# A decoder layer on one core: one exponential moved up on ScalarE, one wait added on GpSimd, one reduction a step later on VectorE

## The reference

```
x = x + self_attention(layernorm(x))          # three softmaxes a row, averaged
x = x + cross_attention(layernorm(x), ctx)    # 16 heads, mask added to the scores
x = x + ffn(layernorm(x))                     # two layers on values rounded to 127 steps
```

## Time and profile before

| what | value |
|---|---|
| median of 3 runs | 1637.55 us (1637.49 to 1640.61) |
| the profiled execution | 1638.86 us, its span 1637.1 us |
| PE busy | 1522.7 us, 93% |
| DVE busy | 1427.2 us, 87% |
| ACT busy | 1218.9 us, 74% |
| POOL busy | 1067.1 us, 65% |
| DMA, over the span | 46 GB/s |
| ACT exponentials, L1174 and L1176 | 256 each, mean 600 and 610 ns |
| POOL exp_lo, L658 | 256, mean 1185 ns |
| POOL idle before exp_lo, waiting for exponentials | 82.8 us |
| DVE waits for normalised x2 before L1516 | 12.0 us in 32 waits |

### The profile page before, as it was taken

How to read it: one execution, slowest core, us unless ns; L and a number is a source line. 1 busy time by engine, 2 the same in 40 slices (tenths; PEclk the granted TensorE clock), 3 DMA queues, 4 the chain that set the end, 5 groups by cost and what they waited for, 6 DMA issues and landing times.

```text
span 1637.1 us, 52303 instructions
## 1 busy us (share of the span) xinstructions
PE 1522.7 (93%) x15938; PEld 1221.6 (75%) x15946; DVE 1427.2 (87%) x6188; ACT 1218.9 (74%) x2497; POOL 1067.1 (65%) x1168
## 2 busy tenths in 40 slices
PE   6589999999999999999999999999999999779897
PEld 5468888888888888888888888888888887532465
DVE  4779999999999999999999999999999996669786
ACT  4767777777777777777777777777777777469875
POOL 3467777777777777777777777777777777642000
PEclk9889999999999999999999999999999999889999
DMA  6000000000000000000000000000000000245154
GB/s 215 4 15 30 29 29 29 29 24 26 29 29 29 29 29 29 29 29 28 23 28 29 29 24 28 29 29 29 29 29 29 29 22 17 91 119 138 39 180 168
DMA packets 92292, 74.67 MB, mean 46 GB/s; under 512 B 20832, under 2 KB 91744, under 8 KB 92256
## 3 DMA queue, kind: packets, MB, share of 16 engines
q1 hardware_dynamic: 91296, 74.08, 14.7%
q10 hardware_dynamic: 960, 0.13, 0.1%
HBM read 45.36 MB, written 25.17 MB: 43 GB/s over the span
## 4 chain that ended last, share of the span: by engine, by line
PE 59%; DVE 18%; ACT 10%; issue 8%; POOL 3%; ACTq 1%; DVEq 1%; DMA 0%; POOLq 0%; SPq 0%
PE banks L124 16%; PE banks L127 13%; PE banks L128 12%; PE banks L914 5%; DVE tile_max L2126 4%; PE banks L934 3%; DVE xn L1342 2%; ACT kv_copy L1154 2%; PE banks L958 2%; ACT normed L1191 2%; PE banks L2030 2%; PE banks L806 2%; DVE g_t_half L1363 2%; DVE stats L1507 1%; POOL rstd L671 1%
## 5 line engine op out<-in xcount | busy, mean ns | idle before, releaser
L658 POOL TENSOR_TENSOR exp_t<-exp_copy,exp_t 128x512 f16<-128x512 f32 x256 | 303.4, 1185 | 141.9 <-ACT exp_copy L1176 82.8
L652 POOL TENSOR_TENSOR shifted<-scores,score_max 128x512 f32<-128x512 f32 x256 | 266.3, 1046 | 131.9 <-DVE score_max L1387 127.2
L1387 DVE CUSTOM_DVE_ANT_0 scores<-banks,mask 128x128 f32<-128x128 f32 x1024 | 232.7, 286 | 6.2 <-PE banks L914 2.9
L1151 ACT ACTIVATE q_t<-banks 128x512 f16<-128x512 f32 x128 | 77.2, 603 | 131.9 <-PE banks L128 131.7
L644 POOL TENSOR_TENSOR v_nat<-kv_copy,v_nat 128x512 f16<-128x512 f32 x128 | 143.8, 1123 | 46.1 <-ACT kv_copy L1154 46.0
L934 PE MATMUL banks<-ident,shifted 128*128 128x128 f32 x1024 | 153.6, 278 | 19.2 <-ACT exp_copy L1176 17.5
L1174 ACT ACTIVATE exp_t<-banks 128x512 f16<-128x512 f32 x256 | 153.6, 600 | 18.5 <-PE banks L934 15.6
L1176 ACT ACTIVATE exp_copy<-banks 128x512 f32<-128x512 f32 x256 | 156.1, 610 | 0.0
L1154 ACT ACTIVATE kv_copy<-banks 128x512 f32<-128x512 f32 x252 | 150.2, 596 | 0.0
L644 POOL TENSOR_TENSOR k_t<-kv_copy,k_t 128x512 f16<-128x512 f32 x124 | 143.9, 1161 | 0.0
L934 PEld LDWEIGHTS banks<-ident,shifted 128*128 128x128 f32 x1024 | 115.3, 142 | 27.6 <-issue 20.6
(11 more groups left out here) (276 smaller groups left out, 5059.3 us busy)
## 6 DMA issues: line engine op xcount, KB each, us to landing
x_in<-in_x_dram SPq DMA_DIRECT2D x32, 256.0 KB, 2.6
ctx_in<-in_ctx_dram SPq DMA_DIRECT2D x32, 256.0 KB, 2.6
x_residual<-x SPq DMA_DIRECT2D x64, 128.0 KB, 1.7
x_normalised<-normed SPq DMA_DIRECT2D x32, 256.0 KB, 2.1
shared<-x_normalised SPq DMA_DIRECT2D x8, 1024.0 KB, 6.9
shared<-x_residual SPq DMA_DIRECT2D x16, 512.0 KB, 3.7
out_dram<-shared SPq DMA_DIRECT2D x16, 512.0 KB, 2.9
mask<-in_fside_Bx1xSxS_dram SPq DMA_DIRECT2D x64, 64.0 KB, 1.9
```

The source lines that it names most:

```text
L652: pool.tensor_tensor(shifted[:, q % 2], scores[:, q % 2], score_max[:, q % 2, :].unsqueeze(2).to_broadcast([P, QUAD, P]), ALU.subtract).th ...
L658: pool.tensor_tensor(exp_t[:, q % 2, LO], exp_copy[:, q % 2], exp_t[:, q % 2, HI], ALU.subtract).then_inc(exp_split, 1)
L1151: op = act.activation(hilo(dst, *at)[HI], src, ACT.Copy)
L1387: op = dve.tensor_tensor_reduce(scores[:, q % 2, h, :], sc_bank(q)[:, tile(h)], mask[:, b, :], 1.0, NEG, ALU.add, ALU.max, score_max[:, q ...
```

## The change

Three edits, in the lists of three engines:

- ScalarE: exponential(3) of the pair before stands ahead of hi(K2) instead of behind it.
- GpSimd: ahead of exp_lo(5), and so ahead of all that follows, it waits for `xn1_ready` of pair i, which VectorE raises at the end of the second instruction that normalises x1. Only in bodies with a front and a back (1 to 31).
- VectorE: `largest_of_x2` of pair i-1 at the end of body i becomes `largest_of_x2` of pair i-2 behind divide(0) in body i. Body 1 has nothing to reduce and is written out ahead of the loop, which now runs from 2 to 30; body 32 reduces pair 30 there and pair 31 at its end.

```diff
--- before.py
+++ after.py
@@ -696,6 +696,9 @@
             if back:
                 shift(6, i - 1)
+                if front:
+
+                    pool.wait_ge(xn1_ready, i + 1)
                 exp_lo(5, i - 1)
                 shift(7, i - 1)
@@ -1203,10 +1206,11 @@
             if early:
                 weights_of["cross_hi"](act, 8, 12)
+            if back:
+                exponential(3, i - 1)
             if front and not early:
                 hi(J_K2, i)
             if back:
-                exponential(3, i - 1)
                 heads_hi(0, i - 1)
                 exponential(4, i - 1)
@@ -1355,7 +1359,7 @@
-        def body(i, front, back, ahead, early=False):
+        def body(i, front, back, ahead, early=False, far=True):
@@ -1557,6 +1561,9 @@
                     row_sums(0, i - 1)
                     divide(0, i - 1)
+                if back and far:
+
+                    largest_of_x2(i - 2)
                 if back and not front:
                     ffn_of["weight_peak"](dve, 0)
@@ -1686,7 +1693,7 @@
                 if front:
                     add_mask(4, i)
-                if back:
+                if back and not front:
                     largest_of_x2(i - 1)
@@ -1696,7 +1703,8 @@
         body(0, True, False, True, True)
-        with dve.Fori(1, PAIRS - 1) as i:
+        body(1, True, True, True, far=False)
+        with dve.Fori(2, PAIRS - 1) as i:
             body(i, True, True, True)
```

## The result

The changed kernel takes 1687.5 us (median of 6 runs, 1686.04 to 1689.37) against 1638.43 for the kernel before: ratio 1.0297, 95% interval 1.0284 to 1.0311. It is slower, as forecast, but by 49 us where 23 were forecast, and outside the range (1638 to 1684). The profiled execution takes 1686.04 us, its span is 1684.2.

What follows compares the result with a forecast made beforehand. TensorE, busy 1229 of 1262 us in the pair loop, bounds it; +0.85 a pair times 30 gives +25.5, with pair 31 and the last body +23.5 on 1638.86: 1662.4, median 1661 us, range 1638 to 1684.

Steps and rivals of the forecast that it cites:

- Keys(1), -0.36: TensorE before keys(1): VectorE's reduction no longer delays the low part of the first probabilities, so keys(1) starts 0.36 us earlier.
- The transposes of quad 5, -0.80: TensorE before quad 5: earlier exponentials free its bank, so its transposes start at 656.11 instead of 656.91.
- The port takes x's normalisation: GpSimd's low half of quad 3 holds VectorE's normalisation of the next x: +1.44 us; x transposes +1.22.
- x's low half, +0.22: fold_value(1) on TensorE waits for x's low half from VectorE, adding 0.22 us to a pair.
- Quad 4, -0.27: GpSimd's low half of quad 4 moves 0.8 us ahead, so the 0.27 us lost before weigh(4) vanishes.
- weigh(5), +0.15: Quad 5's low half on GpSimd runs later, so TensorE's weigh(5) waits, giving 0.15 us back.
- raw_scores: TensorE before raw_scores: x1's normalisation takes 0.73 instead of 1.83 us, so the 0.42 stall goes.
- The sum without the clock: Terms over one pair: +1.22 + 0.22 - 0.27 - 0.42 + 0.15 = +0.90 us, taken as +0.85.
- if weigh(5) doesn't wait: Variant of the pair's sum in which quad 5's low half does not delay TensorE: 0.75 us.
- The extra unrolled body: The body written out on VectorE's queue: costed at 0, as no compute instruction is added in all.
- The clock: Rival, chance 0.16: TensorE's stall lowers the granted clock, 1.7 us in a fifth to two fifths of pairs, 1671 to 1681.
- -0.42 + 0.15: GpSimd's wait for x1's normalisation: raw_scores' 0.42 us stall removed, 0.15 given back at weigh(5).

Runs made afterwards that it cites:

- edit 1: Only VectorE's move of largest_of_x2 behind quad 0's division, against the kernel before: 1636.61 us, ratio 0.9985.
- the filled stall: The changed kernel, with TensorE doing quad 5's four transposes four times in steady pairs: 1659.12 us, ratio 1.0125 to the kernel before.
- edit 2 alone: Only ScalarE's exponential(3) moved ahead of hi(K2), against the kernel before: 1655.41 us, ratio 1.0102.
- edits 2 and 3: ScalarE's moved exponential(3) and GpSimd's wait for xn1_ready, without VectorE's move, against the kernel before: 1660.32 us, ratio 1.0138.
- Edit 3: Only GpSimd's wait for xn1_ready ahead of exp_lo(5), against the kernel before: 1629.46 us, ratio 0.9941.
- edits 1 and 2: VectorE's moved largest_of_x2 and ScalarE's moved exponential(3), without GpSimd's wait, against the kernel before: 1698.36 us, ratio 1.0362.

## Why the prediction was right in kind and wrong in size

- **Keys(1), -0.36: right in place, too small.** The low part of the probabilities moved up and the gap went. Keys(1) starts at 671.13, 0.03 behind the matmul ahead of it and not 0.11 as forecast; that is 649.71 in the time of before, -0.44, and what follows is 0.47 earlier.
- **The transposes of quad 5, -0.80: too small as well.** They start at 677.33, which is 655.91 in the time of before (656.11 forecast): -1.00. The forecast let them start 0.12 behind weigh(2), and they start 0.03 behind it.
- **The port takes x's normalisation: right.** 2.39 us, done at 679.98, in the time of before 658.56 (forecast 658.55); two instructions held, GpSimd ahead at 677.52. The transposes of x are at 680.12, +1.32 (forecast +1.22). TensorE, early at one end and late at the other, stands for 2.15 us and not 1.89 (656.71 to 658.60 in the forecast).
- **x's low half, +0.22: only 0.06.** fold_value(1) is at +1.38 (forecast +1.44). It follows weigh(3) by 0.36 us in both kernels, so it doesn't wait for the low half; the 0.06 come in at K3's start behind the stall.
- **Quad 4, -0.27: right.** weigh(4) is at +1.11 (+1.17).
- **weigh(5), +0.15: there.** Its first row before is

```profile
664.06 0.20 PE L114 MATMUL banks<-v_nat,exp_t 128*128 128x66 f16 x1
```

After, it starts at 686.72, +1.24, where weigh(4) was at +1.11. GpSimd's low half of quad 5 ended at 686.59, so the delay between the two was 0.13 us and not the 0.22 forecast. raw_scores is at +0.74: it gains 0.50 there where 0.42 was forecast.

- **The sum without the clock: 0.72, forecast 0.85.** 1.32 + 0.06 - 0.27 + 0.13 - 0.50 leaves 0.74 at raw_scores, 0.72 at the end of the pair. That it is near the 0.75 given for "if weigh(5) doesn't wait" is luck: weigh(5) does wait. 29 x 0.72 = 21 us. The extra unrolled body was costed at 0; the first period, which begins in it, is 0.33 us longer than the short ones (43.12), and no kernel without edit 1 shows that.
- **The clock: the step that failed.** The sum left it out; it stood as a rival with a chance of 0.16 and 1.7 us for a fifth to two fifths of the pairs. The price of one was near (44.30 - 42.79 = 1.51). The share was 18 of 29, above the upper end of the rival too, and 18 x 1.51 = 27 us; the filled stall measures 28. The two terms make 48 us, which is what the 29 periods grew by (48.6); the medians differ by 49. I set the chance low with the argument that the stall is single with dense work on both sides; but the evidence that I showed, behind the stalls of pair 31, spoke for the fall. The stall was sized short as well (1.89, measured 2.15), and its size matters: 1.68 us cost no fall with edit 2 alone.
- **What was never weighed: that two gains make one loss.** Edit 1 moves TensorE 0.47 up to a wait whose end it does not move (offset 14.64 with it and 14.62 without). So it saves nothing there and makes the stall 2.15 instead of 1.67. With edits 2 and 3 in, edit 1 costs 1687.5 - 1660.3 = 27 us, and all of it is clock, since the short period is 42.79 with it and without; alone it gains 2.
- **Edit 3** was costed as -0.42 + 0.15 in this kernel. On top of edit 2 it shows +0.09 (42.70 and 42.79; ratios 1.0102 and 1.0138): x1's normalisation is free in any case, since the late exponentials hold GpSimd back, and what is left is its price, weigh(5) at offset 21.23 instead of 21.01. It does help alone (-0.37). In the changed kernel its wait is 86.9 us of GpSimd's idle time, most of which costs nothing.

The Trainium skill (SBUF — State Buffer, "Who interferes with whom") says that tensor_reduce on this chip never contends with GpSimd. The trace agrees: before, the reduction of x2 started at 649.21, inside a shift on GpSimd that ran from 649.05 to 650.09, and took 0.69 us, no longer than the 0.67 in its new place.

## What to carry to other kernels

When a wait is removed, look at what its owner does instead of waiting: the engine that stood still may have left a shared port free for another's short, urgent instruction. Before moving work up, find the instruction that sets the end of the next wait; if the move doesn't touch it, the gain becomes a longer stall, and on TensorE a longer stall may cost the clock too, as here between 1.68 and 2.15 us. Where stalls near those that went before a fall of the clock are forecast in every period, the fall belongs in the sum and not among the rivals.

## What the runs showed of the hardware

- A small difference of one stall decided over the clock here. Stalls of 1.67 and 1.68 us once a pair cost it in none of 29 periods (edits 2 and 3, edit 2); stalls of 2.15 us in 18 (all three) and in 28 (edits 1 and 2), so the length alone doesn't decide; the same wait with 1.95 us of transposes ahead of it instead of 0.64, and so 0.84 us idle, in none (the stall filled). One fall costs 1.5 us of a pair.
- VectorE's two normalising instructions take 0.40 us each when free, and up to 1.25 each when a GpSimd instruction with SBUF operands is under way (1.23 and 1.24 in the changed kernel). In the changed kernel the first starts at 677.59 behind GpSimd's 677.52 and ends at 678.82, when GpSimd's has ended (678.68) and its next has begun (678.64); the second then waits for that one (to 679.84) and ends at 679.98.
- A lead of 0.07 us (changed kernel, first instruction) or 0.10 us (edit 1 alone, second) was enough for GpSimd to hold VectorE's instruction for some 0.85 us.
